# A row maximum from the high parts alone, two heads on two halves of TensorE's rows, and an ordered pair of adds, in an attention and feed-forward kernel

## The chip, the cores and the metric

The kernel runs on one core of a Trainium2 chip. The metric is the device time of one execution in microseconds; the time of a kernel is the median of its runs. Before the change it is 1856.97 us, the median of three runs from 1852.95 to 1857.33.

## What is computed

One transformer layer in float32, on x of shape (2, 2048, 256): attention with 8 query heads and 2 key heads of 64 elements, then a feed-forward layer of 1024 with ternary weights, each followed by a layer norm.

```python
qg = x @ Wq;  q, gate = qg[..., :512], qg[..., 512:]
k, v = x @ Wk, x @ Wv                        # 2 key heads of 64, 4 query heads to each
q, k = partial_rope(q), partial_rope(k)      # on the first 16 of 64 elements
scores = einsum('bkgsd,bktd->bkgst', q, k) / 8
attn = softmax(scores)                       # over 2048 keys
out = (attn @ v) * silu(gate) @ Wo
x = layernorm(x + out)
h = bitlinear(x, w_fc) + 0.05 * (x @ v_lr.T @ fast_b.T @ u.T)
x = layernorm(x + bitlinear(relu(h) ** 2, w_proj))
```

The softmax subtracts a number per query row before the exponential. Any number near the row's maximum gives the same quotient; it only has to keep the exponentials in range.

## The kernel before

The two batches are a loop, and each has three stages: a front (projections of all keys and values and of the first queries), the attention, and the feed-forward stage. The change is in the first two.

**Units and steps.** A unit is a pair of heads (`p`, 0 to 3) on a chunk `c` of 512 queries: 16 units per batch. It has 16 steps `t`, one per 128 keys. Every engine has its own function `step` that emits its instructions for step `k` of a chunk; what stands there in what order is what the engine runs, and semaphores tie the engines together. `attention_steps` runs steps 0 to 11, then a loop over the chunks, then the rest.

**High and low parts.** Queries and keys are each split: the part rounded to `fp32r` (`high`) and the rest (`low`). `ka` holds the keys' high part on partitions 0 to 63 and their low part on 64 to 127; `qa` holds the queries' high part twice. So one matmul of 128 rows, `qa` with `ka`, sums high x high and high x low (L547). A second (L550) adds low x high from `qb` and `kb`: rows 0 to 63, and in row 64 the negative maximum (from `mrow`) against a row of ones. That takes the maximum off the scores within PSUM bank `sc`. ScalarE's exponential (L819) writes `probs`, a ring of four slots; `weighted_v` (L562, fp32) multiplies them with the values into `ob`, head 0 in columns (output partitions) 0 to 63, head 1 in 64 to 127. TensorE does that for two steps at a time, in the odd steps.

**The maxima.** The maximum of a unit is worked out ahead, during the unit before it, from scores computed again the other way round: 128 queries on the output partitions, 512 keys along the row. A unit has 8 blocks of queries (4 per head) and 4 chunks of keys: `MAXES` = 32 matmuls of 128 rows (`row_max`, L531). They alternate between the two banks of `mx`; matmul j waits for the reduction of j - 2. VectorE reduces each to a column of `maxp` (`reduce_max`, L1032). `LEAD` = 12 of them are done before the unit before begins; step `t` has two. When all are in, `final_max`, a transpose (L537), `copy_max` and a small DMA bring the numbers to `qb`. In the front, `front_pair` (L701) and `front_reduce` (L1176) do two matmuls and one reduction of 128x1024 at a time, on two pairs of banks.

**The sums.** The denominator is the sum of the exponentials over keys. VectorE adds head 1's half of each `probs` slot to `acc`, GpSimd head 0's (`add_exponentials`, L318 and L322). TensorE then sums over partitions (`denominators`, L573). GpSimd also has the rotary products of a later pair (L294, L295 at step 7, L300 at 8, L306 at 12) and the gating (L923, L926 at 11). VectorE has the reciprocals in four parts at steps 4, 5, 8 and 10 (L1062). TensorE has two projections per unit (L506), after steps 5 and 13. ScalarE also has the gate's exponential (L829), once per unit at step 14.

**DMAs.** SP issues all of them. `place` copies high and low parts from their stage to `ka`, `kb`, `qa` and `qb`; `placed_before` says how many must have landed. A chunk of keys takes four: for either key head one that writes the high part to `ka` and `kb`, and one for the low part.

Of the kernel before, what the change touches and what calls it, by code (L numbers as in the profile page):

```python
# [32 lines left out]
P = 128  # L33
# [13 lines left out]
MAXES = 2 * TILES * KEYCH  # L47
# [4 lines left out]
LEAD = 12  # L52
# [34 lines left out]
def layer_kernel(nc, x, xT, wq, wk, wv, wo, fast_bT, w_fc, w_proj, uT, v_lr, gate, tables, ident_in, out):  # L87
    ctx = ExitStack()
    with ctx:
# [38 lines left out]
        maxp = sb("maxp", [P, 2, MAXES])  # L128
# [59 lines left out]
        ones_set = sem("ones_set")  # L188
        rot_cleared = sem("rot_cleared")
# [89 lines left out]
        def placed_before(stage, b, more=0):  # L279


            slot, local = stage
            local = local + more
            k_at = [f[0] for f in FRONT if f[2] == slot].index("k")
            k_counted = not isinstance(local, int) or local > k_at
            return 96 + 96 * local - 32 * k_counted + b * (96 * per_batch[slot] - 32)
# [21 lines left out]
        def add_exponentials(eng, ops, b, c, k, hd, summed):  # L308
# [3 lines left out]
            cols = slice(hd * CHUNK, (hd + 1) * CHUNK)  # L312
            total, part = acc[:, p % 2, cols], probs[:, k % RING, cols]
# [19 lines left out]
        def _(sp):  # L333
# [30 lines left out]
            def place(stage, b, targets):  # L364
# [5 lines left out]
                for part, hd, dst in targets:  # L370
                    src = raw_words(part[slot][hd * D:(hd + 1) * D])
                    if len(dst.shape) == 3:
                        src = src.unsqueeze(1).broadcast_to([D, 2, CHUNK])
                    sp.dma_start(raw_words(dst), src).then_inc(placed[slot], 16)

            def k_targets(n):
                keys = slice(n * CHUNK, (n + 1) * CHUNK)
                return [t for g in range(KVH) for t in ((high, g, kab[0:D, :, g, keys]), (low, g, ka[D:P, g, keys]))]

            def q_targets(slot):  # L380
                return [t for hd in range(2) for t in (
                    (high, hd, qa[0:D, slot, hd, :]), (high, hd, qa[D:P, slot, hd, :]), (low, hd, qb[0:D, slot, hd, :]))]
# [25 lines left out]
            with sp.Fori(0, BATCH) as b:  # L408
                sp.wait_ge(ones_set, 3)
# [60 lines left out]
        def _(pe):  # L470
# [24 lines left out]
            pe.wait_ge(ones_set, 3)  # L495
# [773 lines left out]
```

## Time and profile before

| what | value |
|---|---|
| median of 3 runs | 1856.97 us |
| span of the profiled execution | 1859.4 us (the page gives no other time for it) |
| TensorE matmuls busy | 1713.8 us, 92% |
| VectorE busy | 1502.4 us, 81% |
| GpSimd busy | 1062.7 us, 57% |
| ScalarE busy | 733.8 us, 39% |
| granted TensorE clock, mean | 0.979 |
| DMA engines' share, whole span | 12% |

Busy shares are means over stages. The attention of a batch is a long row of like units, so the spacing of like instructions says what a unit costs; what ends TensorE's and VectorE's waits within it says why. Matmul records have modelled ends: their starts are what to compare. "PEld" is the loading of weights.

### The profile page before, as it was taken

How to read it: one execution, taken by the hardware profiler on the slowest of the kernel's cores; microseconds unless marked ns; L12 is line 12 of the kernel's file. 1: busy time of each engine (PE TensorE's matmuls, PEld its weight loads, DVE VectorE, ACT ScalarE, POOL GpSimd, SP SyncE). 2: the span in 40 equal slices, each digit the busy share in tenths (PEclk: the TensorE clock that was granted, in tenths of full speed). 3: DMA queues.
4: the chain of work that ended last, by engine and by line, in shares of the span. 5: the costliest groups of instructions: out<-in, count | busy, mean ns of one | idle time of the engine just before them, and what ended most of it. 6: DMA issues, size and time to landing. Idle time of an engine off the chain costs nothing.

```text
span 1859.4 us, 26038 instructions
## 1 busy us (share of the span) xinstructions
PE 1713.8 (92%) x6902; PEld 944.3 (51%) x6902; DVE 1502.4 (81%) x2159; ACT 733.8 (39%) x895; POOL 1062.7 (57%) x764
## 2 busy tenths in 40 slices
PE   5699999999999999999878999999999999999996
PEld 3454444444444444447744544444444444454585
DVE  5688888888888888757858888888888888887577
ACT  2144444444344444444422444434443444434442
POOL 0566666666566665664334666656665666657432
PEclk9899999999999999999979999999999999999998
DMA  4600000000000000010042000000000000000001
GB/s 164 155 22 22 22 22 22 21 21 21 22 21 21 21 19 1 1 74 24 24 123 67 22 22 22 22 22 21 21 21 22 21 21 21 18 1 1 24 23 46
DMA packets 36658, 59.75 MB, mean 32 GB/s; under 512 B 6368, under 2 KB 17008, under 8 KB 36032
## 3 DMA queue, kind: packets, MB, share of 16 engines
q1 hardware_dynamic: 36544, 58.50, 12.1%
q8 instruction: 38, 0.62, 0.1%
q14 instruction: 76, 0.62, 0.1%
HBM read 20.07 MB, written 4.19 MB: 13 GB/s over the span
## 4 chain that ended last, share of the span: by engine, by line
PE 61%; DVE 17%; issue 14%; POOL 3%; DMA 2%; SPq 1%; DVEq 1%; ACT 1%; POOLq 0%; ACTq 0%
PE ob L562 17%; PE mx L531 11%; PE sc L547 9%; PE sc L550 8%; DVE maxp L1032 8%; PE misc L506 6%; DVE acc L322 3%; PE mx L660 3%; POOL acc L322 2%; DMA acc<-in_x 1%; PE misc L573 1%; DVE maxp L1176 1%; PE ob L675 1%; PE misc L675 1%; PE sc L627 1%
## 5 line engine op out<-in xcount | busy, mean ns | idle before, releaser
L322 POOL TENSOR_TENSOR acc<-acc,probs 128x512 f32<-128x512 f32 x448 | 625.1, 1395 | 370.9 <-ACT probs L819 346.0
L819 ACT ACTIVATE probs<-sc 128x1024 f32<-128x1024 f32 x512 | 522.6, 1024 | 642.0 <-PE sc L550 633.8
L1032 DVE TENSOR_REDUCE maxp<-mx 128x1 f32<-128x512 f32 x936 | 614.4, 677 | 186.8 <-PE mx L531 182.5
L322 DVE TENSOR_TENSOR acc<-acc,probs 128x512 f32<-128x512 f32 x448 | 516.1, 1152 | 26.3 <-ACT probs L819 25.7
L562 PE MATMUL ob<-probs,v_sb 128*64 128x512 f32 x2048 | 501.1, 610 | 0.5 <-ACT probs L819 0.5
L531 PE MATMUL mx<-kab,qa 128*128 128x512 f32 x936 | 403.9, 452 | 58.9 <-DVE maxp L1032 58.9
L547 PE MATMUL sc<-qa,kab 128*128 128x512 f32 x1024 | 325.6, 399 | 0.1
L550 PE MATMUL sc<-qb,kab 65*128 65x512 f32 x1024 | 321.7, 395 | 0.0
L531 PEld LDWEIGHTS mx<-kab,qa 128*128 128x128 f32 x936 | 175.3, 187 | 278.0 <-issue 133.0
L562 PEld LDWEIGHTS ob<-probs,v_sb 128*64 128x64 f32 x2048 | 124.6, 136 | 241.0 <-issue 227.2
L547 PEld LDWEIGHTS sc<-qa,kab 128*128 128x128 f32 x1024 | 192.2, 189 | 53.4 <-issue 17.5
L550 PEld LDWEIGHTS sc<-qb,kab 65*128 65x128 f32 x1024 | 194.2, 190 | 45.9
L506 PE MATMUL misc<-xT_sb,wqg_sb 128*128 (+1 forms) x248 | 123.7, 621 | 5.1 <-ACT wp_scale L777 2.8
L1062 DVE RECIPROCAL oge<-oge 128x128 f32<-128x128 f32 x128 | 119.5, 937 | 0.1
L962 POOL TENSOR_TENSOR raw_sb<-raw_sb 128x512 f32<-128x512 f32 x32 | 38.7, 1211 | 139.0 <-ACT raw_sb L855 137.9
L318 POOL TENSOR_TENSOR acc<-probs 128x512 f32<-128x512 f32 x32 | 41.9, 1308 | 126.8 <-ACT probs L819 126.8
L506 PEld LDWEIGHTS misc<-xT_sb,wqg_sb 128*128 128x128 f32 x248 | 42.3, 190 | 85.3 <-issue 85.3
L660 PE MATMUL mx<-low_sb,kab 128*128 128x512 f32 x256 | 71.6, 402 | 0.6 <-ACT low_sb L850 0.6
L923 POOL TENSOR_TENSOR oge<-oge 128x512 f32<-128x512 f32 x32 | 42.9, 1341 | 38.8 <-DVE oge L1062 38.8
L829 ACT ACTIVATE oge<-misc 128x512 f32<-128x512 f32 x32 | 19.1, 598 | 105.2 <-PE misc L506 105.2
L306 POOL TENSOR_TENSOR low_sb<-raw_sb,high_sb 128x512 fp32r<-128x512 f32 x32 | 49.7, 1555 | 13.2 <-ACT high_sb L795 13.2
L627 PE MATMUL sc<-og,wo_sb 128*128 128x512 f32 x128 | 56.5, 594 | 0.0
(126 smaller groups left out, 1435.5 us busy)
## 6 DMA issues: line engine op xcount, KB each, us to landing
qa<-high_sb SPq DMA_DIRECT2D x128, 128.0 KB, 2.3
qb<-low_sb SPq DMA_DIRECT2D x64, 128.0 KB, 2.3
tables_sb<-in_tables SPq DMA_DIRECT2D x34, 128.0 KB, 2.4
xT_sb<-in_xT SPq DMA_DIRECT2D x2, 2048.0 KB, 9.5
acc<-in_x SPq DMA_DIRECT2D x8, 512.0 KB, 4.3
out_y<-acc SPq DMA_DIRECT2D x8, 512.0 KB, 3.2
rot_sb<-raw_sb SPq DMA_DIRECT2D x72, 32.0 KB, 1.9
probs<-in_tables SPq DMA_DIRECT2D x4, 512.0 KB, 3.9
```

The source lines that it names most:

```text
L306: eng.tensor_tensor(low[slot], raw[slot], high[slot].bitcast(F32), ALU.subtract).then_inc(low_done[slot], 1)
L322: ops.tensor_tensor(total, total, part, ALU.add).then_inc(summed, 1)
L506: mm = nc.tensor.matmul(bank[:, :], w[:, h, col:col + P], xT_sb[:, h, bass.ds(chunk * CHUNK, CHUNK)], start=(h == 0), stop=(h == HC - 1))
L531: nc.tensor.matmul(mx[:, j % 2, :], qa[:, p % PAIRS, hd, st * P:(st + 1) * P], ka[:, p % PAIRS // 2, kc * CHUNK:(kc + 1) * CHUNK], start=T ...
L547: nc.tensor.matmul(sc[:, 2 * (k % 2) + hd, :], ka[:, kv, keys], qa[:, p % PAIRS, hd, :], start=True, stop=False)
L550: mm = nc.tensor.matmul(sc[:, 2 * (k % 2) + hd, :], kb[0:D + 1, kv, keys], qb[0:D + 1, p % PAIRS, hd, :], start=False, stop=True)
L562: mm = nc.tensor.matmul(ob[hd * D:(hd + 1) * D, :], v_sb[:, t, kv * D:(kv + 1) * D], probs[:, k % RING, hd * CHUNK:(hd + 1) * CHUNK], star ...
L627: mm = nc.tensor.matmul(sc[:, h, :], wo_sb[:, p, h * P:(h + 1) * P], og[:, c * PAIRS + p, :], start=(p == 0), stop=(p == PAIRS - 1))
L660: mm = nc.tensor.matmul(mx[:, j % 2, :], w[:, h, j * P:(j + 1) * P], x1t[:, h, :], start=(w is w_high and x1t is x1_high and h == 0), stop ...
L819: nc.scalar.activation(probs[:, k % RING, :].rearrange("p (h n) -> p h n", h=2), sc[:, 2 * (k % 2):2 * (k % 2) + 2, :], ACT.Exp, scale=flo ...
L1032: nc.vector.tensor_reduce(maxp[:, p % 2, column:column + 1], mx[:, j % 2, :], AX_X, ALU.max)\
L1062: nc.vector.reciprocal(e_sb[:, cols], e_sb[:, cols]).then_inc(recip_done, 1)
```

## The change

There are two parts.

1. **The maxima.** They are worked out from high x high alone, 64 rows instead of 128. A matmul of head 0 uses partitions 0 to 63 (`qa[0:D]`, `ka[0:D]`), one of head 1 partitions 64 to 127 (`qa[D:P]`, and `kb[D:P]`, which now holds the keys' high part there). The two write the two banks of `mx`, and this is one pass (`pass_of_two_heads`); a unit has 16. A pass waits for the reduction of the pass before; VectorE reduces both banks in one instruction. A step has one pass: in even steps ahead of the scores, in odd steps between scores and `weighted_v`. `LEAD` is 6 passes. For this `kb` and `qb` change layout: row 0 holds the ones and the negative maximum, rows 1 to 63 zeros, rows 64 to 127 the high keys and the low queries, and the second score matmul takes 128 rows. VectorE clears `kb[0:64]` and GpSimd `qb[0:64]` once at the start, and a chunk of keys is placed by six DMAs. The maximum that is subtracted thus leaves out the scores' low parts; the scores themselves keep them.
2. **The adds.** GpSimd's add of step k waits until VectorE's of the same step is done (`sum_b`).

```diff
-MAXES = 2 * TILES * KEYCH
+PASSES = TILES * KEYCH
-LEAD = 12
+LEAD = 6
...
-        def add_exponentials(eng, ops, b, c, k, hd, summed):
+        def add_exponentials(eng, ops, b, c, k, hd, summed, after=None):
...
+            if after is not None and t >= 1:
+                eng.wait_ge(after, done(n + 1))
...
-                return [t for g in range(KVH) for t in ((high, g, kab[0:D, :, g, keys]), (low, g, ka[D:P, g, keys]))]
+                return [t for g in range(KVH) for t in (
+                    (high, g, ka[0:D, g, keys]), (low, g, ka[D:P, g, keys]), (high, g, kb[D:P, g, keys]))]
...
+            def pass_of_two_heads(banks, pair, j):
+
+                queries = slice(j % TILES * P, (j % TILES + 1) * P)
+                keys = slice(j // TILES * CHUNK, (j // TILES + 1) * CHUNK)
+                nc.tensor.matmul(banks[:, 0, :], qa[0:D, pair, 0, queries], ka[0:D, pair // 2, keys],
+                                 start=True, stop=True)
+                return nc.tensor.matmul(banks[:, 1, :], qa[D:P, pair, 1, queries], kb[D:P, pair // 2, keys],
+                                        start=True, stop=True)
...
-                pe.wait_ge(maxed, done(unit * MAXES + j - 1))
-                nc.tensor.matmul(mx[:, j % 2, :], qa[:, p % PAIRS, hd, st * P:(st + 1) * P],
-                                 ka[:, p % PAIRS // 2, kc * CHUNK:(kc + 1) * CHUNK],
-                                 start=True, stop=True).then_inc(max_ready, 1)
+                pe.wait_ge(maxed, done(unit * PASSES + j))
+                pass_of_two_heads(mx, p % PAIRS, j).then_inc(max_ready, 1)
...
-                    mm = nc.tensor.matmul(sc[:, 2 * (k % 2) + hd, :], kb[0:D + 1, kv, keys],
-                                          qb[0:D + 1, p % PAIRS, hd, :], start=False, stop=True)
+                    mm = nc.tensor.matmul(sc[:, 2 * (k % 2) + hd, :], kb[:, kv, keys],
+                                          qb[:, p % PAIRS, hd, :], start=False, stop=True)
...
+                    if t % 2 == 0:
+                        look_ahead(LEAD + t)
                     if not (isinstance(c, int) and c == NCH - 1 and k == PAIRS * STEPS - 1):
                         scores(b, c, k + 1)
-                    look_ahead(LEAD + 2 * t)
-                    if t % 2 == 0:
-                        look_ahead(LEAD + 2 * t + 1)
+                    if t % 2:
+                        look_ahead(LEAD + t)
                     if t % 2:
                         weighted_v(b, c, k - 1)
                         weighted_v(b, c, k)
...
-                    if t % 2:
-                        look_ahead(LEAD + 2 * t + 1)
...
-                    add_exponentials(pool, nc.gpsimd, b, c, k, 0, sum_a)
+                    add_exponentials(pool, nc.gpsimd, b, c, k, 0, sum_a, sum_b)
...
+            nc.gpsimd.memset(qb[0:D, :, :, :].bitcast(F32), 0.0).then_inc(ones_set, 1)
...
-            nc.vector.memset(kb[D:D + 1, :, :].bitcast(F32), 1.0).then_inc(ones_set, 1)
+            nc.vector.memset(kb[0:D, :, :].bitcast(F32), 0.0).then_inc(kb_cleared, 1)
+            dve.wait_ge(kb_cleared, 1)
+            nc.vector.memset(kb[0:1, :, :].bitcast(F32), 1.0).then_inc(ones_set, 1)
...
-                nc.vector.tensor_reduce(maxp[:, p % 2, column:column + 1], mx[:, j % 2, :], AX_X, ALU.max)\
-                  .then_inc(maxed, 1)
+                nc.vector.tensor_reduce(two_columns(p, j), mx[:, :, :], AX_X, ALU.max).then_inc(maxed, 1)
```

What stands in a row on the engines moves at three places. TensorE, before, in an even and an odd step (scores are the pairs with `sc`, maxima those with `mx`; register instructions set up waits); the even step's own scores stand just ahead of these rows:

```order
L530 REGISTER_ALU
L531 MATMUL mx<-kab,qa 128x512
L530 REGISTER_ALU
L531 MATMUL mx<-kab,qa 128x512
L545 REGISTER_ALU
L547 MATMUL sc<-qa,kab 128x512 x2
L550 MATMUL sc<-qb,kab 128x512 x2
L530 REGISTER_ALU
L531 MATMUL mx<-kab,qa 128x512
L562 MATMUL ob<-probs,v_sb 64x512 x2
L558 REGISTER_ALU
L562 MATMUL ob<-probs,v_sb 64x512 x2
```

TensorE now, both steps whole:

```order
L538 REGISTER_ALU
L526 MATMUL mx<-kab,qa 128x512
L528 MATMUL mx<-kab,qa 128x512
L553 MATMUL sc<-qa,kab 128x512 x2
L556 MATMUL sc<-qb,kab 128x512 x2
L553 MATMUL sc<-qa,kab 128x512 x2
L556 MATMUL sc<-qb,kab 128x512 x2
L538 REGISTER_ALU
L526 MATMUL mx<-kab,qa 128x512
L528 MATMUL mx<-kab,qa 128x512
L568 MATMUL ob<-probs,v_sb 64x512 x4
```

Four separate maxima have become two passes, one on either side of `ob`, and the scores of two steps stand together.

VectorE, before, from the last part of an odd step on (reductions have `mx`, adds have `acc`):

```order
L1032 TENSOR_REDUCE maxp<-mx 128x1 [waits max_ready]
L1030 REGISTER_ALU
L1032 TENSOR_REDUCE maxp<-mx 128x1 [waits max_ready]
L1030 REGISTER_ALU
L1032 TENSOR_REDUCE maxp<-mx 128x1 [waits max_ready]
L320 REGISTER_ALU
L322 TENSOR_TENSOR acc<-acc,probs 128x512 [waits sum_b,probs_ready]
```

VectorE now:

```order
L1039 REGISTER_ALU
L1040 TENSOR_REDUCE maxp<-mx 128x2 [waits max_ready]
L323 TENSOR_TENSOR acc<-acc,probs 128x512 [waits sum_b,probs_ready]
L1039 REGISTER_ALU
L1040 TENSOR_REDUCE maxp<-mx 128x2 [waits max_ready]
L323 TENSOR_TENSOR acc<-acc,probs 128x512 [waits sum_b,probs_ready]
```

Reductions came three before one add and one before the next; now reduction and add alternate.

GpSimd, the first two adds of a batch, before:

```order
L315 ISA
L317 REGISTER_ALU [waits probs_ready]
L318 TENSOR_TENSOR acc<-probs 128x512 [waits den_ready]
L320 REGISTER_ALU
L322 TENSOR_TENSOR acc<-acc,probs 128x512 [waits sum_a,probs_ready]
```

And now:

```order
L313 ISA
L318 REGISTER_ALU [waits probs_ready,sum_b]
L319 TENSOR_TENSOR acc<-probs 128x512 [waits den_ready]
L313 REGISTER_ALU
L323 TENSOR_TENSOR acc<-acc,probs 128x512 [waits sum_a,probs_ready,sum_b]
```

Nothing moved there; each add has one more wait, for VectorE's count.

## Rows read from the trace of the kernel before

**Rows 1.** The page's busy times of the engines, whole span.
```profile
PE 1713.8 (92%) x6902; PEld 944.3 (51%) x6902; DVE 1502.4 (81%) x2159; ACT 733.8 (39%) x895; POOL 1062.7 (57%) x764
```

**Rows 2.** ScalarE in order of time: start us, us, engine, line, operation (idle before).
```profile
130.69 0.60 ACT L829 ACTIVATE oge<-misc 128x512 f32<-128x512 f32 x1 [3.03 <-PE misc L506]
...
689.43 0.60 ACT L829 ACTIVATE oge<-misc 128x512 f32<-128x512 f32 x1 [2.93 <-PE misc L506]
```

**Rows 3.** One unit: its stretch, length, busy us (instructions) per engine, clock, DMA share, GB/s.
```profile
409.36:455.60 46.24, 44.26 (x175) 22.75 (x174) 40.31 (x54) 19.14 (x22) 29.68 (x22) 1.00 0.09 22
```

**Rows 4.** TensorE in order of time, in that unit: columns as in rows 2.
```profile
411.95 1.94 PE L562 MATMUL ob<-probs,v_sb 128*64 128x512 f32 x8
413.82 0.50 PE L531 MATMUL mx<-kab,qa 128*128 128x512 f32 x1
414.16 0.62 PE L547 MATMUL sc<-qa,kab 128*128 128x512 f32 x2
414.62 0.62 PE L550 MATMUL sc<-qb,kab 65*128 65x512 f32 x2
...
416.81 1.94 PE L562 MATMUL ob<-probs,v_sb 128*64 128x512 f32 x8
418.57 1.03 PE L573 MATMUL misc<-acc,ones 128*64 128x512 f32 x4
...
422.52 1.94 PE L562 MATMUL ob<-probs,v_sb 128*64 128x512 f32 x8
...
427.97 1.94 PE L562 MATMUL ob<-probs,v_sb 128*64 128x512 f32 x8
429.84 1.98 PE L506 MATMUL misc<-xT_sb,wqg_sb 128*128 x4
...
434.56 1.94 PE L562 MATMUL ob<-probs,v_sb 128*64 128x512 f32 x8
```

**Rows 5.** TensorE in order of time, two maxima in a row.
```profile
425.65 0.40 PE L531 MATMUL mx<-kab,qa 128*128 128x512 f32 x1
426.38 0.50 PE L531 MATMUL mx<-kab,qa 128*128 128x512 f32 x1 [0.33 <-DVE maxp L1032]
```

**Rows 6.** VectorE and GpSimd in order of time, in that unit.
```profile
411.54 1.27 POOL L322 TENSOR_TENSOR acc<-acc,probs 128x512 f32<-128x512 f32 x1 [1.25 <-ACT probs L819]
...
411.88 1.48 DVE L322 TENSOR_TENSOR acc<-acc,probs 128x512 f32<-128x512 f32 x1
...
413.89 0.67 DVE L322 TENSOR_TENSOR acc<-acc,probs 128x512 f32<-128x512 f32 x1
...
435.37 1.72 POOL L294 TENSOR_TENSOR raw_sb<-raw_sb,tables_sb 128x512 f32<-128x512 f32 x1
...
436.48 1.16 DVE L322 TENSOR_TENSOR acc<-acc,probs 128x512 f32<-128x512 f32 x1
...
440.50 0.94 DVE L1062 RECIPROCAL oge<-oge 128x128 f32<-128x128 f32 x1
```

**Rows 7.** Groups by line and shape, whole span: count, busy us, mean ns, idle before.
```profile
L1032 DVE TENSOR_REDUCE maxp<-mx 128x1 f32<-128x512 f32 x936 | 614.4, 677 | 186.8 <-PE mx L531 182.5 <-issue 1.6
...
L322 DVE TENSOR_TENSOR acc<-acc,probs 128x512 f32<-128x512 f32 x448 | 516.1, 1152 | 26.3 <-ACT probs L819 25.7
```

**Rows 8.** Groups of the weight loads, whole span.
```profile
L531 PEld LDWEIGHTS mx<-kab,qa 128*128 128x128 f32 x936 | 175.3, 187 | 278.0 <-issue 133.0 <-DVE maxp L1032 117.7
L562 PEld LDWEIGHTS ob<-probs,v_sb 128*64 128x64 f32 x2048 | 124.6, 136 | 241.0 <-issue 227.2 <-ACT probs L819 13.9
```

**Rows 9.** The front's reductions (group), the first clearing, a key DMA, the first maximum.
```profile
L1176 DVE TENSOR_REDUCE maxp<-mx 128x2 f32<-128x1024 f32 x22 | 26.8, 1219 | 25.8 <-PE mx L701 25.8
...
3.05 3.47 DVE L971 MEMSET kab<- 1x4096 f32 x1 [3.05 <-issue]
...
55.39 0.67 SPq L374 DMA_DIRECT2D kab<-low_sb  x1
...
59.41 1.21 PE L701 MATMUL mx<-kab,qa 128*128 128x512 f32 x2 [6.52 <-DMA kab<-low_sb]
```

More of the change, by code:

```diff
@@ L283, in placed_before @@
             local = local + more
-            k_at = [f[0] for f in FRONT if f[2] == slot].index("k")
-            k_counted = not isinstance(local, int) or local > k_at
-            return 96 + 96 * local - 32 * k_counted + b * (96 * per_batch[slot] - 32)
+            return 96 * (1 + local + b * per_batch[slot])
         def rope(eng, stage, b):
@@ L695, in front_pair @@
                 def front_pair(p, i):
-                    pe.wait_ge(maxed, done((b * UNITS + p) * MAXES + (2 * (i - 1) if p or i else 0)))
-                    for half in range(2):
-                        hd, st, n = i % TILES // 2, i % 2 * 2 + half, i // TILES
-                        mm = nc.tensor.matmul(MAX_PAIRS[i % 2][:, half, :], qa[:, p, hd, st * P:(st + 1) * P],
-                                              ka[:, p // 2, n * CHUNK:(n + 1) * CHUNK], start=True, stop=True)
-                    mm.then_inc(max_ready, 2)
+                    pe.wait_ge(maxed, done((b * UNITS + p) * PASSES + (i - 1 if p or i else 0)))
+                    pass_of_two_heads(MAX_PAIRS[i % 2], p, i).then_inc(max_ready, 1)
                 def front_maxima(n):
@@ L730, in _ @@
                 max_transpose(b, 0, 0)
-                for i in range(2, LEAD // 2):
+                for i in range(2, LEAD):
                     front_pair(1, i)
@@ L1024, in _, with two_columns @@
             last.then_inc(setup_dve, 1)
+            def two_columns(p, j):
+                column = j % TILES * KEYCH + j // TILES
+                return maxp[:, p % 2, column:column + PASSES + 1:PASSES]
             def reduce_max(b, c, p, j):
@@ L1029, in reduce_max @@
                     dve.wait_ge(max8_done, done(unit - 1))
-                dve.wait_ge(max_ready, done(unit * MAXES + j + 1))
-                column = j % (2 * TILES) * KEYCH + j // (2 * TILES)
-                nc.vector.tensor_reduce(maxp[:, p % 2, column:column + 1], mx[:, j % 2, :], AX_X, ALU.max)\
-                  .then_inc(maxed, 1)
+                dve.wait_ge(max_ready, done(unit * PASSES + j + 1))
+                nc.vector.tensor_reduce(two_columns(p, j), mx[:, :, :], AX_X, ALU.max).then_inc(maxed, 1)
             def final_max(b, c, p):
                 unit = b * UNITS + c * PAIRS + p
-                dve.wait_ge(maxed, done((unit + 1) * MAXES))
+                dve.wait_ge(maxed, done((unit + 1) * PASSES))
                 dve.wait_ge(mt_ready, done(unit))
@@ L1068, in look_ahead @@
                     def look_ahead(j):
[L1069 removed]
+                        ahead = 1 + j // PASSES
                         if exists(c, p, ahead):
[L1071 to L1072 removed]
+                            reduce_max(b, c, p + ahead, j % PASSES)
+                            if j == PASSES - 1:
                                 final_max(b, c, p + 1)
[L1075 to L1077 removed]
+                    look_ahead(LEAD + t)
                     add_exponentials(dve, nc.vector, b, c, k, 1, sum_b)
@@ L1185, in _ @@
                         rope_low(nc.vector, front(s), b)
-                for i in range(MAXES // 2):
+                for i in range(PASSES):
                     front_reduce(0, i)
                 final_max(b, 0, 0)
-                for i in range(LEAD // 2):
+                for i in range(LEAD):
                     front_reduce(1, i)
```

34 lines of the change are left out of this document (11 added, 23 removed).

## The prediction

> **What bounds the kernel now.** I read the busy shares first, then the spacing of like rows, then the order of time on TensorE, VectorE and GpSimd. TensorE is busy 92% of the span [rows 1]. The gate's exponential, once per unit (one pair of heads on one chunk of queries), starts at 130.69 us and twelve units later at 689.43 [rows 2]: 46.56 us per unit; the one whose rows I show takes 46.24, with TensorE busy 44.26, VectorE 40.31 and GpSimd 29.68 [rows 3]. These spacings hold for 13 units per batch, 26 in all; the last three of a batch have fewer maxima or none, and shrink. So nearly two thirds of the span, 26 x 46.56 = 1211 us, is this unit, repeated.
>
> What is TensorE's own work in it? The visits to `ob` start at 411.95, 416.81, 422.52, 427.97 and 434.56 [rows 4]. The tightest spacing is 4.86: two steps with nothing late. The next holds the denominators too, 5.71, so these cost 0.85. 434.56 - 427.97 = 6.59 holds a projection, so that costs 1.73. A unit has 8 double steps, one pair of denominators and two projections: 38.88 + 0.85 + 3.46 = 43.2 us. The other 3.05 us of 46.24 are lost. Where: 427.97 - 422.52 = 5.45 is 0.59 too long, and there the maximum at 426.38 waited for VectorE's reduction [rows 5]. So TensorE is the bound and VectorE holds it up for 7% of the time.
>
> Why is VectorE late, when it is busy 87%? [Rows 6]: GpSimd adds from 411.54 to 412.81; VectorE's add begins at 411.88, takes 1.48 and ends 0.55 after GpSimd's. At 413.89, GpSimd idle, the same add takes 0.67. At 435.37 GpSimd's rotary product takes 1.72, to 437.09, and VectorE's add ends at 437.64, again 0.55 later. So **an add of VectorE that begins during an operation of GpSimd stands still until that ends**. Over the run it means 1152 ns [rows 7]; 0.48 us of each is standing, 15 x 0.48 = 7.2 us per unit.
>
> **The change part by part.**
>
> *The maxima on TensorE.* Before, a double step has 8 score matmuls, 4 maxima and `ob`. Pitch: 414.16 to 414.62 holds two, 0.23 each [rows 4]. `ob` is 8 records; the denominators, 4 records in a mode already open, cost 0.85, so 0.213 each and 1.71 for `ob`. 12 x 0.233 + 1.71 = 4.51 of 4.86; the remaining 0.35 is the trip into column halves and out, 0.175 per change of mode. That halves can run together is visible there: a projection has 4 records of 128 columns in about 1.7 us, `ob` 8 of 64 columns in as much [rows 4]. After, a double step has two passes, each a switch in and a switch out: four changes of mode against two. One pass with both halves together costs 0.235. How dear a change into row halves is, no row shows. Bounds: nothing (weights loaded ahead) and 0.25 (see below). I take the column trip's 0.175, and add 0.013, since three of the four changes load 128 columns of weights and before one of two did: loads take 187 and 136 ns for 128 and 64 [rows 8]. Sum: 8 x 0.233 + 2 x 0.235 + 1.71 + 4 x 0.188 = 4.80 us, against 4.86. **Half the maximum matmuls disappear, and the switches eat that.** The Trainium skill (TensorEngine Tiling (Array Packing), Key Properties) says that a change of tiling mode, not of tile, drains TensorE. It gives no price; with a price of nothing for the row changes the double step would be 4.40, with the row's price 4.80. By the rule I keep the latter. The unit: 38.4 + 0.85 + 2 x (1.71 + 0.19) = 43.05 us, against 43.2.
>
> *The maxima on VectorE.* 32 reductions of 0.677 [rows 7] become 16 over two banks, 1.219 each [rows 9]; instructions overlap their neighbour by 0.07, so 19.4 against 18.4: 1.0 us less. The handshake gets tighter: a pass writes both banks and waits for the reduction of the pass before, where a matmul waited for the one before the last.
>
> *GpSimd waits for VectorE's add.* Its add k starts after VectorE's add k, and VectorE has a reduction of 1.15 before add k+1. GpSimd's add takes 1.27 [rows 6]. So add k+1 meets at most its last 0.2: 0.48 of standing becomes 0.1, some 5 us of VectorE's time per unit. Behind GpSimd's wait are queued its rotary steps, the gating and the `probs` slot that the exponential reuses four steps on; GpSimd is busy 29.7 of 46 and the slot has about one double step to spare, so these cost nothing. If GpSimd fell a double step behind, ScalarE's exponential would wait and TensorE's scores with it.
>
> *What is late next.* I put the steps in order by hand, from: reduction 1.15, free add 0.61, reciprocal 0.87 (0.94 [rows 6] less the overlap), 0.4 from a pass's start to its reduction, 0.17 from a reduction's end to TensorE's next pass, passes 2.5 and 2.3 us apart. Between two passes reduction and add take 1.76 and fit. At steps 4 and 5 two reciprocals push VectorE 0.3 behind, hidden by the projection. At 7 and 8 GpSimd does its add and three rotary operations of 1.72. VectorE's add of step 8 stands some 1.3, the reciprocal follows, the reduction of 9 ends 1.0 late, and pass 10 waits 1.0. Add 9 or 10 is caught once more, with step 10's reciprocal behind it: 0 to 1.2, I take 0.65. Steps 11 to 3 have room. Lost: 1.65 us per unit in place of 3.05. **Unit: 43.05 + 1.65 = 44.7 us against 46.24, 26 x 1.5 = 39 us saved.**
>
> *Beside it.* The front's passes number as many as its pairs of maxima did, reduced at 1.22 as before: nothing. A chunk of keys takes six DMAs for four, 0.67 us of SP each [rows 9]; the first maximum waits 6.52 for just these. 1.3 for the first chunk and about 0.7 for the later ones, per batch: 4 us. The second clearing of `kab` costs VectorE 3.5 at the start [rows 9], ahead of a setup in which it later waits for TensorE; GpSimd's of `qb` comes before it has other work; 0 to 3.5, I take 1, near the end that a wait hides. The second score matmul has 128 rows for 65 at the same pitch: nothing. Sum: -39 + 5 = -34.
>
> The profiled execution has a span of 1859.4 us, 0.13% above the median of 1856.97. I apply the difference to the median: 1857 - 34 = **1823 us**.
>
> **The rivals.** (a) *Changes into row halves are free* (weights loaded ahead). Double step 4.40, unit 39.5; VectorE then is the limit and more is lost, say the 3.05 of now: 42.6, 26 x 3.65 = 95 saved, 1767 us. Against: the change into column halves, which also only loads other weights, is not free. (b) *The second half starts late*: its 128 columns load after the first's, 64 columns cost 51 ns [rows 8], so 0.10 per pass, 1.6 per unit, of which 0.5 come out of waiting. Saved 10, less 5: 1852 us. The Trainium skill (TensorE: Matmul & The Clock Gate, LDWEIGHTS) gives columns / 1.2 as a load's nanoseconds. An estimate from it is 107 ns per pass, the same rival. (c) *The halves run one after the other.* Each pass costs 0.23 more, 3.7 per unit; waits shrink to 1.0, unit 47.8, 26 x 1.55 + 5 = 45 lost, **1902 us, slower**. It is one price: after exceeds before as soon as a pass with its two changes costs over 0.15 more than I take, a change over 0.25. For it: no row has row halves. Against: column halves do overlap. The change not taking hold on GpSimd would show as adds of 1.15 still; the wait is on the very count that VectorE's add raises, so I give it no chance of its own.
>
> **The numbers.** Forecast 0.45, (a) 0.13, (b) 0.20, (c) 0.22. My own case spans 1795 to 1850, since a change dearer or cheaper by 0.03 is 25 us. The range goes to 1772, leaving out half of (a), and to 1896, leaving out half of (c). A measurement of this kernel tells 0.3%, 5.6 us, from nothing. Faster: 0.43 + 0.13 + 0.09 of (b) = 0.65. Same: 0.02 + 0.09 = 0.11. Slower: 0.22 + 0.02 of (b) = 0.24.
>
> **What would show it.** VectorE's add near 0.75 us in the mean; GpSimd's adds starting just behind it. The two matmuls of a pass starting together; 4.8 us from `ob` to `ob` in steps with nothing late; units of 44.7. Waits of TensorE for reductions at steps 9 to 12 only. I am wrong if the tightest `ob` spacing is under 4.5 or over 5.1, or if waits for reductions stay at 3 us per unit.

## The result, and the profile after

The changed kernel takes 1773.99 us in the median of four runs (1773.88 to 1777.63), the kernel before 1856.03 (1852.95 to 1857.33) beside it. The ratio is 0.9567 [0.9551 to 0.9584]: 4.3% faster, 2 us inside the fast end of the range (1772). I had forecast 1823: the gain is 82 us where I gave 34.

The page of the kernel after: first the busy times of the whole span, as in [rows 1], then the shares of the chain that ended last:

```profile
PE 1674.5 (94%) x6902; PEld 858.6 (48%) x6902; DVE 1378.8 (78%) x1692; ACT 710.5 (40%) x895; POOL 1030.5 (58%) x765
...
PE 75%; DVE 12%; issue 7%; POOL 3%; DMA 2%; ACT 1%; SPq 0%; DVEq 0%; POOLq 0%; ACTq 0%
```

TensorE's busy time fell by 39 us and its share rose from 92 to 94%; VectorE lost 124 us of busy time. ScalarE's gate exponentials of the kernel after, in order of time, as in [rows 2]:

```profile
133.10 0.60 ACT L830 ACTIVATE oge<-misc 128x512 f32<-128x512 f32 x1 [3.12 <-PE misc L506]
...
656.01 0.60 ACT L830 ACTIVATE oge<-misc 128x512 f32<-128x512 f32 x1 [3.11 <-PE misc L506]
```

(656.01 - 133.10) / 12 = 43.58 us per unit, where it was 46.56. A plain unit, away from the border of a chunk, takes 43.52, where it was 46.24 and I expected 44.7. The first gate begins 2.4 us later than before. One unit of the kernel after, columns as in [rows 3]:

```profile
402.06:445.58 43.52, 43.15 (x175) 19.96 (x174) 36.43 (x38) 18.32 (x22) 28.79 (x21) 1.00 0.10 23
```

TensorE waits 43.52 - 43.15 = 0.37 us in it, where the unit before left 1.98 open; VectorE is busy 36.43 in place of 40.31. TensorE in order of time in that unit, as in [rows 4]:

```profile
402.06 1.94 PE L568 MATMUL ob<-probs,v_sb 128*64 128x512 f32 x8
...
407.26 0.49 PE L526 MATMUL mx<-kab,qa 64*128 64x512 f32 x1
407.26 0.50 PE L528 MATMUL mx<-kab,qa 64*128 64x512 f32 x1
407.69 1.94 PE L568 MATMUL ob<-probs,v_sb 128*64 128x512 f32 x8
409.56 0.50 PE L526 MATMUL mx<-kab,qa 64*128 64x512 f32 x1
409.56 0.49 PE L528 MATMUL mx<-kab,qa 64*128 64x512 f32 x1
409.99 0.74 PE L553 MATMUL sc<-qa,kab 128*128 128x512 f32 x2
...
412.45 1.94 PE L568 MATMUL ob<-probs,v_sb 128*64 128x512 f32 x8
...
419.13 1.94 PE L568 MATMUL ob<-probs,v_sb 128*64 128x512 f32 x8
...
423.92 1.94 PE L568 MATMUL ob<-probs,v_sb 128*64 128x512 f32 x8
426.23 0.50 PE L526 MATMUL mx<-kab,qa 64*128 64x512 f32 x1 [0.37 <-DVE maxp L1040]
...
429.14 1.94 PE L568 MATMUL ob<-probs,v_sb 128*64 128x512 f32 x8
431.00 0.27 PE L543 MATMUL misc<-ident,max 128*8 128x128 f32 x1
...
434.10 1.94 PE L568 MATMUL ob<-probs,v_sb 128*64 128x512 f32 x8
```

407.69 to 412.45 is 4.76 us, a double step with nothing late. The two matmuls of a pass start together (407.26, 409.56), and `ob` begins 0.43 us behind the pass. The one wait of the matmuls for a reduction is at 426.23; 431.00 is the transpose of the finished maxima. (Busy time has modelled ends, so a unit's loss is better read from these spacings, as in the prediction: 0.7 us now, see below, where it was 3.05.) VectorE, then GpSimd, around that wait, as in [rows 6]:

```profile
421.54 1.23 DVE L1040 TENSOR_REDUCE maxp<-mx 128x2 f32<-128x1024 f32 x1 [0.48 <-PE mx L528]
422.69 1.54 DVE L323 TENSOR_TENSOR acc<-acc,probs 128x512 f32<-128x512 f32 x1
424.15 0.94 DVE L1069 RECIPROCAL oge<-oge 128x128 f32<-128x128 f32 x1
425.01 1.16 DVE L1040 TENSOR_REDUCE maxp<-mx 128x2 f32<-128x1024 f32 x1
...
421.15 1.29 POOL L323 TENSOR_TENSOR acc<-acc,probs 128x512 f32<-128x512 f32 x1 [1.19 <-DVE acc L323]
422.39 1.29 POOL L293 TENSOR_TENSOR raw_sb<-raw_sb,tables_sb 128x512 f32<-128x512 f32 x1
423.64 1.73 POOL L294 TENSOR_TENSOR rot_sb<-rot_sb,tables_sb 128x512 f32<-128x512 f32 x1
```

The groups of reductions and adds, as in [rows 7]:

```profile
L323 POOL TENSOR_TENSOR acc<-acc,probs 128x512 f32<-128x512 f32 x448 | 602.8, 1346 | 365.8 <-DVE acc L323 353.4 <-POOL acc L323 6.8 <-ACT probs L820 5.6
L1040 DVE TENSOR_REDUCE maxp<-mx 128x2 f32<-128x1024 f32 x468 | 567.1, 1212 | 232.3 <-PE mx L528 225.8 <-issue 2.5
...
L323 DVE TENSOR_TENSOR acc<-acc,probs 128x512 f32<-128x512 f32 x448 | 422.8, 944 | 23.5 <-ACT probs L820 22.6
```

VectorE's adds fell from 1152 to 944 ns, not to the 0.75 us I had named. 353.4 of the 365.8 us that GpSimd idles before its adds now end with VectorE's add: that is the new wait at work.

**Where 87 us of span came from** (1859.4 to 1772.1, by the gate's exponentials of both batches). The 24 spacings of full units fell from 1119.4 to 1045.7 us: 73.7. The last three of a batch fell from 120.2 to 114.4 us, 11.7 in both batches together. The stretch between the batches gave 2.9 and the end 1.4; the start took 2.4 more.

### The profile page after: what moved, and what is told of

Read it like the earlier page. It is cut to its first block, busy times and chain, and to the rows that moved or that the text cites. A ratio compares the mean times of both kernels' runs of the same rounds, so it can differ in the third digit from the quotient of the medians.

```text
span 1772.1 us, 24588 instructions
## 1 busy us (share of the span) xinstructions
PE 1674.5 (94%) x6902; PEld 858.6 (48%) x6902; DVE 1378.8 (78%) x1692; ACT 710.5 (40%) x895; POOL 1030.5 (58%) x765
## 4 chain that ended last, share of the span: by engine, by line
PE 75%; DVE 12%; issue 7%; POOL 3%; DMA 2%; ACT 1%; SPq 0%; DVEq 0%; POOLq 0%; ACTq 0%
PE ob L568 23%; PE sc L553 14%; PE sc L556 11%; PE mx L526 11%; PE misc L506 6%; PE mx L665 3%; DVE acc L323 2%; DVE maxp L1040 2%; POOL acc L323 2%; PE misc L579 1%; DVE maxp L1178 1%; PE sc L632 1%; PE ob L680 1%; DMA acc<-in_x 1%; DVE oge L1069 1%
## 5 line engine op out<-in xcount | busy, mean ns | idle before, releaser
L323 POOL TENSOR_TENSOR acc<-acc,probs 128x512 f32<-128x512 f32 x448 | 602.8, 1346 | 365.8 <-DVE acc L323 353.4
L1040 DVE TENSOR_REDUCE maxp<-mx 128x2 f32<-128x1024 f32 x468 | 567.1, 1212 | 232.3 <-PE mx L528 225.8
L820 ACT ACTIVATE probs<-sc 128x1024 f32<-128x1024 f32 x512 | 501.2, 1025 | 574.5 <-PE sc L556 574.5
L323 DVE TENSOR_TENSOR acc<-acc,probs 128x512 f32<-128x512 f32 x448 | 422.8, 944 | 23.5 <-ACT probs L820 22.6
L553 PE MATMUL sc<-qa,kab 128*128 128x512 f32 x1024 | 351.1, 424 | 0.0
L556 PE MATMUL sc<-qb,kab 128*128 128x512 f32 x1024 | 320.8, 394 | 0.0
L526 PE MATMUL mx<-kab,qa 64*128 64x512 f32 x490 | 248.4, 507 | 32.3 <-DMA kab<-high_sb 12.4
L528 PE MATMUL mx<-kab,qa 64*128 64x512 f32 x490 | 247.9, 506 | 0.0
L526 PEld LDWEIGHTS mx<-kab,qa 64*128 64x128 f32 x490 | 91.1, 186 | 295.3 <-issue 153.1
L556 PEld LDWEIGHTS sc<-qb,kab 128*128 128x128 f32 x1024 | 193.6, 189 | 45.7
L528 PEld LDWEIGHTS mx<-kab,qa 64*128 64x128 f32 x490 | 91.0, 186 | 0.0
L788 ACT COPY raw_sb<-misc 128x512 f32<-128x512 f32 x32 | 18.8, 587 | 102.0 <-PE misc L506 100.3
```

Of the source, the lines that this page charges most:

```text
L323: ops.tensor_tensor(total, total, part, ALU.add).then_inc(summed, 1)
L526: nc.tensor.matmul(banks[:, 0, :], qa[0:D, pair, 0, queries], ka[0:D, pair // 2, keys], start=True, stop=True)
L528: return nc.tensor.matmul(banks[:, 1, :], qa[D:P, pair, 1, queries], kb[D:P, pair // 2, keys], start=True, stop=True)
L553: nc.tensor.matmul(sc[:, 2 * (k % 2) + hd, :], ka[:, kv, keys], qa[:, p % PAIRS, hd, :], start=True, stop=False)
L556: mm = nc.tensor.matmul(sc[:, 2 * (k % 2) + hd, :], kb[:, kv, keys], qb[:, p % PAIRS, hd, :], start=False, stop=True)
L820: nc.scalar.activation(probs[:, k % RING, :].rearrange("p (h n) -> p h n", h=2), sc[:, 2 * (k % 2):2 * (k % 2) + 2, :], ACT.Exp, scale=flo ...
```

## The experiments

Ratios are to the kernel before, with 95% intervals. "Unit" is the spacing of the gate's exponential in the middle of the first batch; the add is the mean of VectorE's 448 `acc` adds in the profile.

| kernel | median us | ratio | unit us | add ns |
|---|---|---|---|---|
| before | 1856 | 1 | 46.24 | 1152 |
| after | 1773.99 | 0.9567 [0.9551, 0.9584] | 43.52 | 944 |
| e1_wait_alone | 1804.60 | 0.9728 [0.9707, 0.9750] | 44.32 | 956 |
| e2_no_wait | 1769.42 | 0.9540 [0.9520, 0.9560] | 43.11 | 967 |
| e3_full_rows | 1766.65 | 0.9519 [0.9498, 0.9540] | 43.34 | 883 |
| e4_same_half | 1880.58 | 1.0132 [1.0108, 1.0156] | 46.67 | 912 |
| e5_recips_early | 1767.16 | 0.9518 [0.9498, 0.9538] | 43.24 | 915 |
| e6_full_rows_no_wait | 1764.27 | 0.9490 [0.9472, 0.9507] | 43.04 | 1019 |
| e7_two_reductions | 1765.92 | 0.9500 [0.9480, 0.9520] | 43.13 | 1015 |
| e8_pass_behind_scores | 1921.74 | 1.0347 [1.0327, 1.0367] | 48.70 | 1040 |
| e9_old_code_new_order | 1790.22 | 0.9637 [0.9616, 0.9657] | 44.10 | 1065 |
| e10_new_order_recips | 1789.51 | 0.9632 [0.9612, 0.9652] | 43.88 | 1090 |
| e11_new_order_wait | 1780.40 | 0.9583 [0.9564, 0.9603] | 43.66 | 946 |
| e12_full_rows_recips | 1786.31 | 0.9624 [0.9609, 0.9639] | 43.90 | 1010 |

### Which part of the change brings it: the wait, or the maxima?

**e1_wait_alone** is the kernel before with GpSimd's wait alone:

```diff
-        def add_exponentials(eng, ops, b, c, k, hd, summed):
+        def add_exponentials(eng, ops, b, c, k, hd, summed, after=None):
...
+            if after is not None and t >= 1:
+                eng.wait_ge(after, done(n + 1))
...
-                    add_exponentials(pool, nc.gpsimd, b, c, k, 0, sum_a)
+                    add_exponentials(pool, nc.gpsimd, b, c, k, 0, sum_a, sum_b)
```

> The kernel before with the second part of the change alone: GpSimd's add waits for VectorE's. Theory A (most of the gain is VectorE's freed time, because its adds no longer stand behind GpSimd's): adds of VectorE near 0.95 us in the mean instead of 1.15, TensorE's waits for reductions from 3.05 to about 1 us per unit, unit 44.2, time near 1800 us. Theory B (most of the gain is the new order and the halved maxima, the wait is minor): the time stays above 1840 us.

**e2_no_wait** is the kernel after without it:

```diff
-                    add_exponentials(pool, nc.gpsimd, b, c, k, 0, sum_a, sum_b)
+                    add_exponentials(pool, nc.gpsimd, b, c, k, 0, sum_a)
```

> The changed kernel without GpSimd's wait: the maxima part alone. Theory A: adds of VectorE back at 1.15 us, 3 us of waits per unit again behind 42.8 us of work, unit 45.8, time near 1835 us. Theory B: within 10 us of the changed kernel, below 1785 us.

Measured: the wait alone takes off 51 us, the other part alone 86 or 87, both together 82. So theory A came true for the one kernel and theory B for the other, and the two parts do not add up: the maxima's part brings everything by itself, and on top of it the wait costs 5 us (the intervals just overlap, but the runs of the two kernels don't, and the unit is 43.52 us with it and 43.11 without). The group of VectorE's adds in e1_wait_alone:

```profile
L1034 DVE TENSOR_REDUCE maxp<-mx 128x1 f32<-128x512 f32 x936 | 616.2, 679 | 226.9 <-PE mx L533 214.4 <-issue 9.0
L324 POOL TENSOR_TENSOR acc<-acc,probs 128x512 f32<-128x512 f32 x448 | 587.3, 1311 | 443.9 <-DVE acc L324 441.2 <-POOL acc L324 2.7
...
L324 DVE TENSOR_TENSOR acc<-acc,probs 128x512 f32<-128x512 f32 x448 | 428.2, 956 | 23.5 <-ACT probs L821 22.8
```

956 ns: the wait frees the adds in the old order just as well as in the new. TensorE's waits for reductions of VectorE (its matmuls in the attention, whole span) were 58.9 us before, 28.8 in e1_wait_alone and 9.2 in the kernel after. Both parts draw on the same 3 us of waiting per unit, and it can be given back only once.

### What do row halves bring on TensorE?

**e3_full_rows** keeps the passes, their order and the wait, but each matmul has 128 rows (high x high and high x low, as before):

```diff
-                nc.tensor.matmul(banks[:, 0, :], qa[0:D, pair, 0, queries], ka[0:D, pair // 2, keys],
+                nc.tensor.matmul(banks[:, 0, :], qa[:, pair, 0, queries], ka[:, pair // 2, keys],
...
-                return nc.tensor.matmul(banks[:, 1, :], qa[D:P, pair, 1, queries], kb[D:P, pair // 2, keys],
+                return nc.tensor.matmul(banks[:, 1, :], qa[:, pair, 1, queries], ka[:, pair // 2, keys],
```

> The changed kernel, but each matmul of a pass takes all 128 rows (the maxima of the scores with their low parts, as before), so there are no changes into row halves and no overlap. Theory A (a change of mode costs about 0.18 us, so the two that a pass adds nearly eat the 0.235 us it saves): ob to ob 4.86 us where nothing is late, unit up by 0.5 to 0.8, time 1785 to 1797 us. Theory C (row halves cost nothing to enter and their overlap is the gain): ob to ob near 5.2 us, time near 1860 us.

**e4_same_half** puts both matmuls of a pass on partitions 0 to 63, so that they can't run at once:

```diff
-                return nc.tensor.matmul(banks[:, 1, :], qa[D:P, pair, 1, queries], kb[D:P, pair // 2, keys],
+                return nc.tensor.matmul(banks[:, 1, :], qa[0:D, pair, 1, queries], ka[0:D, pair // 2, keys],
```

> The changed kernel, but head 1's matmul of a pass also uses partitions 0 to 63 (the same numbers lie there), so the two matmuls cannot run together while the changes of mode stay. All theories that have the halves overlap: each pass 0.21 to 0.24 us longer, ob to ob 5.2 us, unit up by 3.0 to 3.7 us, time 1850 to 1875 us. If the records' equal starts were only modelled and the halves ran in turn: no change, 1774 us.

Measured: I had expected full rows to be slower than row halves (1785 to 1797 us), but they are 7 us faster. Two halves in turn cost 107 us (1880.58 against 1773.99), 10.5 of them ahead of the first gate, which starts at 143.60. TensorE's visits to `ob` in e3_full_rows, one double step with nothing late and one with a projection:

```profile
446.76 1.94 PE L568 MATMUL ob<-probs,v_sb 128*64 128x512 f32 x8
...
451.62 1.94 PE L568 MATMUL ob<-probs,v_sb 128*64 128x512 f32 x8
...
458.14 1.94 PE L568 MATMUL ob<-probs,v_sb 128*64 128x512 f32 x8
```

and in e4_same_half:

```profile
403.87 1.94 PE L568 MATMUL ob<-probs,v_sb 128*64 128x512 f32 x8
...
409.09 1.94 PE L568 MATMUL ob<-probs,v_sb 128*64 128x512 f32 x8
```

The double step is 4.76 us in halves, 451.62 - 446.76 = 4.86 in full rows (4.85 elsewhere in the unit), 5.22 on one half. 5.22 - 4.76 = 0.46 is 0.23 per pass, one matmul's pitch: the halves do run together, and this is the price of rival (c), measured. From 4.76 the price of a change of mode follows as in the prediction: 4.76 - 8 x 0.233 - 2 x 0.235 - 1.71 = 0.72, four changes, 0.18 each in the mean, where I took 0.188 (this rests on the 1.71 that the prediction worked out for `ob` itself). So 0.46 us of matmuls are saved and 0.36 paid for two more changes. The Trainium skill says that a change of tiling mode drains TensorE while a change of tile does not (TensorEngine Tiling (Array Packing), Key Properties); the trace agrees, at 0.18 us a change. The projections take much of this back: 458.14 - 451.62 = 6.52 us with a projection in full rows, 419.13 - 412.45 = 6.68 in halves. What is left is 0.2 us a unit, and the double step with the transpose takes that too: it is 434.10 - 429.14 = 4.96 in halves, 0.2 over the plain one, where in full rows it is 4.83 (e6_full_rows_no_wait), no longer than the plain one. The two kernels without GpSimd's wait show the balance: 43.11 us a unit in halves (e2_no_wait), 43.04 in full rows (e6_full_rows_no_wait). So **the halves save nothing in a unit**. With the wait the kernel after even loses: 43.52 to 43.34 through longer waits (5 us a run), and its first gate is 3.5 us later, on which more below.

### The best of the parts, and its limit

**e6_full_rows_no_wait** has both edits, of e3_full_rows and of e2_no_wait.

> The changed kernel with 128-row matmuls in its passes (computing the maxima of the scores with their low parts) and without GpSimd's wait: what is left of the change is the pass of two banks, its place in the order and one reduction for both. Runs so far: row halves cost 7 us, the wait 5 us. If these add up: 1760 to 1764 us. If both act through the same waits of TensorE: 1765 us or more.

Measured: 1764.27 us, the lowest median here (e7_two_reductions and e3_full_rows, within 2.4 us of it, can't be told from it). A unit of it:

```profile
406.47:449.52 43.05, 43.05 (x174) 23.01 (x173) 36.83 (x39) 18.35 (x22) 30.02 (x22) 1.00 0.10 23
```

TensorE is busy 43.05 of 43.05 us. Those ends are modelled, but the starts say the same: its double steps are 4.83 to 4.92 us with nothing late, 5.69 with the denominators and 6.53 with a projection. Nothing that is done for VectorE or GpSimd can shorten this unit further; it is TensorE's own work, and in it no matmul waits for a reduction.

### The order of the work, or the merged instructions?

**e7_two_reductions** is e6_full_rows_no_wait with two reductions of one bank each for the one of two:

```diff
-                nc.vector.tensor_reduce(two_columns(p, j), mx[:, :, :], AX_X, ALU.max).then_inc(maxed, 1)
+                column = j % TILES * KEYCH + j // TILES
+                nc.vector.tensor_reduce(maxp[:, p % 2, column:column + 1], mx[:, 0, :], AX_X, ALU.max)
+                nc.vector.tensor_reduce(maxp[:, p % 2, column + PASSES:column + PASSES + 1], mx[:, 1, :],
+                                        AX_X, ALU.max).then_inc(maxed, 1)
```

> As e6_full_rows_no_wait, but VectorE reduces the two banks of a pass in two instructions of one bank. Theory D (the even order is the gain: reduction and add alternate, passes 2.3 to 2.5 us apart): VectorE has 1.0 us more per unit, most of it hidden, at most 20 us slower than e6. Theory E (the one instruction for two banks is the gain): the waits of 3 us per unit are back, above 1810 us.

**e8_pass_behind_scores** is e6_full_rows_no_wait with the pass of an even step behind its scores, not ahead of them, so that the passes are no longer evenly spaced:

```diff
-                    if t % 2 == 0:
-                        look_ahead(LEAD + t)
...
-                    if t % 2:
-                        look_ahead(LEAD + t)
+                    look_ahead(LEAD + t)
```

> As e6_full_rows_no_wait, but the pass of an even step also stands behind the scores, as the maxima stood before, so passes are 1.2 and 3.7 us apart. Theory D: a pass needs 0.4 us, a reduction of 1.2 and 0.2 to start the next, 1.8 us in all, so each second pass waits 0.6 us or more; 5 us per unit, time near 1880 us. Theory E: no change against e6, within 10 us.

**e9_old_code_new_order** is the kernel before, single matmuls of 128 rows and single reductions, moved to where the passes stand: in even steps both maxima ahead of the scores, in odd steps both ahead of `weighted_v`, and on VectorE both reductions ahead of the add. No wait on GpSimd. On TensorE:

```diff
+                    if t % 2 == 0:
+                        look_ahead(LEAD + 2 * t)
+                        look_ahead(LEAD + 2 * t + 1)
                     if not (isinstance(c, int) and c == NCH - 1 and k == PAIRS * STEPS - 1):
                         scores(b, c, k + 1)
-                    look_ahead(LEAD + 2 * t)
-                    if t % 2 == 0:
+                    if t % 2:
+                        look_ahead(LEAD + 2 * t)
                         look_ahead(LEAD + 2 * t + 1)
...
-                    if t % 2:
-                        look_ahead(LEAD + 2 * t + 1)
```

> The kernel before with its order alone changed: two maxima ahead of the scores in even steps, two between scores and the values' matmuls in odd ones, and on VectorE two reductions ahead of each add. Four separate maxima, two banks in turn, 128 rows, four DMAs for a chunk of keys, no wait of GpSimd. Theory D (the order is the gain): the unit comes down to TensorE's own work, 43.0 to 43.3 us, time 1758 to 1768 us. If the pass of two banks, with one semaphore for two matmuls, is needed for it: above 1790 us.

Measured: splitting the reduction costs nothing that can be told (1765.92 against 1764.27, the intervals overlap). The uneven order costs 157 us, 5.7 us a unit where I had expected 5: its passes start by turns 1.9 and 3.6 us or more apart, and the second finds VectorE still in the reduction of the first. Three of its passes in order of time, then the reduction between the first two, then the groups of its first matmuls:

```profile
427.15 0.39 PE L526 MATMUL mx<-kab,qa 128*128 128x512 f32 x1
...
429.09 0.50 PE L526 MATMUL mx<-kab,qa 128*128 128x512 f32 x1 [0.41 <-DVE maxp L1037]
...
432.65 0.40 PE L526 MATMUL mx<-kab,qa 128*128 128x512 f32 x1
...
427.81 1.23 DVE L1037 TENSOR_REDUCE maxp<-mx 128x2 f32<-128x1024 f32 x1 [3.04 <-PE mx L528]
...
L526 PE MATMUL mx<-kab,qa 128*128 128x512 f32 x490 | 224.4, 458 | 122.9 <-DVE maxp L1037 101.3 <-DMA kab<-high_sb 12.7 <-DVE maxp L1175 8.4
...
L526 PEld LDWEIGHTS mx<-kab,qa 128*128 128x128 f32 x490 | 92.4, 189 | 247.7 <-DVE maxp L1037 208.3 <-DVE maxp L1175 16.4 <-issue 13.5
```

101.3 us of idle time end with a reduction, and the weight loads ahead of them spend 208.3 in the same wait. The new order in the old code, e9_old_code_new_order, takes off 66 us of the 82. So **the place of the maxima is enough for most of the gain**: pairs of them, evenly spaced, each followed on VectorE by one add. It is not the only way to most of it, since the wait alone brought 51. And it is not all: I had expected 1758 to 1768 us of e9_old_code_new_order, and its 1790 us is where I had put a kernel that needs the pass of two banks. Where its other 24 us against e7_two_reductions are lost is shown at the end. The kernel moves the maxima on TensorE and the reductions on VectorE together; the second without the first was not run.

### The reciprocals, with and without the wait

In my sum one wait of 1.65 us per unit was left because two reciprocals of VectorE (steps 8 and 10) fall among GpSimd's long products. Four kernels take them to steps 4 to 7; one of these also tries the wait in the new order of the old code:

```diff
-RECIP_STEPS = (4, 5, 8, 10)
+RECIP_STEPS = (4, 5, 6, 7)
```

**e5_recips_early** is the kernel after with this line.

> The changed kernel with the four reciprocals at steps 4, 5, 6 and 7 instead of 4, 5, 8 and 10. Theory A (what TensorE still waits, some 0.5 us per unit at steps 9 to 12, comes of reciprocals behind an add that stands still while GpSimd does its rotary products): the waits go, unit 43.0, time 1760 to 1766 us. Rival: the stall moves to another step, within 4 us of 1774 us.

**e10_new_order_recips** is e9_old_code_new_order with it.

> As e9_old_code_new_order, with the reciprocals at steps 4, 5, 6 and 7. If e9 has no waits left, this gives nothing: within 3 us of e9. If the later units of a batch (42.4 and 40.5 us in e6) still wait for VectorE, up to 3 us less.

**e11_new_order_wait** is e10_new_order_recips with GpSimd's wait of e1_wait_alone. Its expectation speaks of e9_old_code_new_order alone, but its edit holds the early reciprocals too, so e10_new_order_recips is the kernel to compare it with.

> As e9_old_code_new_order, with GpSimd's add waiting for VectorE's. VectorE's add goes from about 1.02 to about 0.88 us, but TensorE has no waits left to give back in a unit, so nothing is gained: within 3 us of e9, or up to 5 us slower, as the wait cost 5 us between e2 and the changed kernel.

**e12_full_rows_recips** is e6_full_rows_no_wait with the line.

> As e6_full_rows_no_wait, with the reciprocals at steps 4, 5, 6 and 7. The steady unit of e6 has no wait left (43.05 us, TensorE busy 43.05), so it stays; the units 14 and 15 of a batch, 42.4 and 40.5 us there against 41.2 and 39.2 with early reciprocals, can give back up to 2.5 us per batch. Time 1758 to 1764 us. If an add of VectorE falls behind one of GpSimd's that starts together with it, as in e9, up to 1 us per unit is lost instead: up to 1790 us.

Measured: with the wait, the early reciprocals gain 7 us (e5_recips_early against the kernel after). Without it they gain nothing in the old code (e10_new_order_recips against e9_old_code_new_order: its full units are 0.2 us shorter, but the first two of the last three of a batch are 2.2 us longer together) and lose 22 us on e6_full_rows_no_wait, the second of the two outcomes that I had named. VectorE in a unit of e12_full_rows_recips:

```profile
419.89 1.39 DVE L323 TENSOR_TENSOR acc<-acc,probs 128x512 f32<-128x512 f32 x1
421.20 0.94 DVE L1069 RECIPROCAL oge<-oge 128x128 f32<-128x128 f32 x1
422.06 1.16 DVE L1040 TENSOR_REDUCE maxp<-mx 128x2 f32<-128x1024 f32 x1
423.14 1.08 DVE L323 TENSOR_TENSOR acc<-acc,probs 128x512 f32<-128x512 f32 x1
```

Two adds stand behind GpSimd, 1.39 and 1.08 us where a free one takes 0.67, with a reciprocal between them, and the reduction in the middle is late. The wait gains 9 us in the new order of the old code (e11_new_order_wait against e10_new_order_recips), where I had expected nothing or a loss; beside late reciprocals it was not tried in that order. In the new code it loses 2 us with full rows and 5 with halves, both at the edge of what the intervals tell apart. With it the time depends less on where VectorE's other work stands: these kernels suggest that, and don't prove it for others.

## Why the prediction was right or wrong

**Right.** The bound (TensorE) and what held it up (VectorE's reductions). *Double step 4.80*: 4.76, and the tightest before was 4.86. *Half the maximum matmuls disappear, and the switches eat that*: 0.46 saved and 0.36 eaten in a double step, and the rest in projections and transpose. The unit's own work, *43.05*, is 8 x 4.76 + 0.87 + 2 x 1.92 = 42.8, or 43.0 with the 0.2 of the transpose. Rivals (a), (b) and (c) fall: changes of mode are not free, the second half starts within 0.01 us of the first, and the halves don't run in turn. That the time came near (a)'s 1767 is no point for it: its double step would be 4.40. (One sum of the rivals is off. A margin of 34 us is 0.08 us for each pass of 26 units, and 0.12 where waits shrink to 1.0 as in (c); the prediction says 0.15.)

**The step that failed is "Lost: 1.65 us per unit in place of 3.05".** The spacings of `ob` in the kernel after (5.63, 4.76, 6.68, 4.79, 5.22, 4.96, 6.71, 4.77; their starts run from 402.06 to 445.58) leave 43.52 - 42.8 = 0.7 us. (0.87 is what the denominators add, 1.92 what a projection does.) 0.46 of it is in the double step with the wait (5.22), and 0.2 is the transpose (4.96), which is work and not waiting. I had let GpSimd's three rotary operations all take 1.72, VectorE's add of step 8 stand to their end, pass 10 wait 1.0 and another add be caught for 0.65. What happened is in the rows of VectorE and GpSimd above: the first product took 1.29, VectorE's add of 422.69 stood for it alone and ended at 424.23, 0.55 behind its end, while the second product ran its 1.73; reciprocal and reduction (425.01) followed, and pass 10 waited 0.37. The second catch did not come at add 9 or 10 (0.77 and 0.68 us); add 11, at 430.74, took 1.26, but no pass waited for it. Such an order by hand rests on who starts first, within tenths of a microsecond, and I had set each uncertain one against the change. The same step was too kind to the adds: *0.48 of standing becomes 0.1*, but 944 ns is 0.27 above a free add. So less was lost although more was left standing, and the number of the adds was no measure of the loss.

**The scope was the second error: "26 x 1.5".** The last three units of the two batches gained 11.7 us, 8.7 more than the 1.5 that I had counted for one of them in each batch, and the spacings at the borders of chunks, 47.2 to 49.0 before, are 43.7 to 43.8 after, 7.7 us more than the plain unit tells. *Beside it: +5* was -2: first gate +2.4, rest -4.3. The six DMAs and the clearings in it cost nothing that shows: e3_full_rows has them too, and its first gate, at 129.57, is 1.1 us earlier than that of the kernel before.

Of the 53 us by which the span's gain of 87 exceeds 34, the wait (1.65 to 0.7 in 24 units) is thus 23, TensorE's work (43.05 to 42.8) 6, the borders 8, the last units 9 and what stands beside 7.

**The reason was credited wrongly.** I put the gain down to *a free add* and the wait on GpSimd. In the old order that holds, as e1_wait_alone shows with 51 us. But in the kernel after the wait is not needed: e2_no_wait and e9_old_code_new_order show that the order brings most of the gain without it, one reduction, one add, one reduction, one add, at equal distances. In this order the adds that still stand no longer hold TensorE up: VectorE's mean add is 1019 ns in e6_full_rows_no_wait, 75 more than in the kernel after, and yet in its plain unit no matmul waits for a reduction.

## What to carry to other kernels

Work out first whether the producer's hand-overs are evenly spaced and whether the consumer's work between two of them fits the gap; moving instructions that already exist was worth 66 us here, the rest of the rewriting another 16 to 26. When two edits draw on the same wait, price them together: the gain of the second is what the first left over. And a matmul on half the rows pays for itself only if its neighbours are in that mode as well: at 0.18 us a change, two changes (0.36) cost more than the 0.23 us that one matmul of 512 columns takes.

## What the runs showed that I had not expected

**A tie between two adds decides a microsecond.** In e9_old_code_new_order both engines start an add at 425.94 (VectorE, then GpSimd; then TensorE in the same stretch):

```profile
425.94 1.83 DVE L322 TENSOR_TENSOR acc<-acc,probs 128x512 f32<-128x512 f32 x1
...
425.94 1.28 POOL L322 TENSOR_TENSOR acc<-acc,probs 128x512 f32<-128x512 f32 x1
...
426.81 1.94 PE L562 MATMUL ob<-probs,v_sb 128*64 128x512 f32 x8
429.23 1.09 PE L531 MATMUL mx<-kab,qa 128*128 128x512 f32 x2 [0.48 <-DVE maxp L1033]
...
432.58 1.94 PE L562 MATMUL ob<-probs,v_sb 128*64 128x512 f32 x8
```

GpSimd's takes its free time, VectorE's ends 0.55 us after it. TensorE's next maxima wait for the reductions behind it, and the double step takes 432.58 - 426.81 = 5.77 us in place of 4.86. That is the only one of this unit that is late, and its 0.9 us are nearly all by which the unit exceeds that of e7_two_reductions (44.10 to 43.13), 23 of the 24 us between the two kernels. In e6_full_rows_no_wait VectorE's starts 0.05 us sooner:

```profile
416.96 0.68 DVE L323 TENSOR_TENSOR acc<-acc,probs 128x512 f32<-128x512 f32 x1
...
417.01 1.75 POOL L323 TENSOR_TENSOR acc<-acc,probs 128x512 f32<-128x512 f32 x1
```

Now VectorE's takes 0.68 and GpSimd's takes 1.75, and GpSimd has the room. In e7_two_reductions both start at 417.86, and VectorE's takes 0.68 and GpSimd's 1.81: of two adds that start together either can be the free one, and why it is the one or the other is not shown. The Trainium skill says that the two engines share a pair of ports under an exclusive lock, which VectorE needs for an instruction with two SBUF inputs and which the first to start holds for its whole instruction (SBUF — State Buffer, SBUF: two separate sides). The trace agrees, both ways round, with the 0.55 us beside it.

**The granted clock in the front.** From 80 to 100 us, with the last front passes, the kernel after is granted 0.57 (the last but two columns are the clock, DMA share and GB/s):

```profile
80.00:100.00 20.00, 16.30 (x45) 7.46 (x45) 15.75 (x17) 3.69 (x4) 4.44 (x4) 0.57 0.38 86
```

e3_full_rows, the same program with 128 rows in a pass:

```profile
80.00:100.00 20.00, 15.69 (x59) 8.35 (x60) 16.71 (x18) 5.22 (x6) 5.04 (x5) 1.00 0.33 74
```

All four kernels with 64-row passes show 0.57 to 0.60 there (after, e2_no_wait, e4_same_half, e5_recips_early), so they spend most of the stretch at the lower of the two levels, 1.2 GHz. The five with the same front in full rows (e3, e6, e7, e8, e12) show 1.00, and the five with the old front 0.74 to 1.00. The mean clock of the whole span says the same in every execution: 0.969 to 0.978 in 16 of kernels with 64-row passes, 0.980 to 0.988 in 22 of those five in full rows. Of the front passes of the kernel after between 82 and 94 us each matmul takes 0.79 us, where later ones take 0.50. Its first gate starts at 133.10 us, that of e3_full_rows at 129.57. That is part of the 7 us by which full rows win. Why the clock differs, no run here takes apart.
